# A self-attention block and a channel-correlation norm on one core: the second image's products moved into image 0, a third tile split on GpSimd, and the last image finished in three column pieces

## The chip, the cores and the metric

One core of one Trainium2 chip. The metric is the device time of one execution in microseconds (us), taken over repeated runs. TensorE (PE) does the matmuls, VectorE (DVE), ScalarE (ACT) and GpSimd (POOL) the rest, SyncE (SP) issues most DMAs.

## The reference

The input has 8 images of 128 channels by 1024 pixels, in float32.

```python
x_f = einsum('oc,bcn->bon', Wf, xf) + bf      # 16 x 1024, as x_g; x_h is 128 x 1024
s = einsum('bci,bcj->bij', x_f, x_g)          # 1024 x 1024 an image
beta = softmax(s, axis=-1)
y = x + gamma * einsum('bci,bij->bcj', x_h, beta)
x_n = y / max(norm(y over pixels), 1e-12)
cos = einsum('bcn,bdn->cd', x_n, x_n) / B     # needs all 8 images
idx = top_k(-abs(cos), 4)                     # per channel, 3 partners beside itself
# sums and squares over a channel and its partners give mean and var of each image
out = gn_gamma * (y - mean) * rsqrt(var + 1e-5) + gn_beta
```

## The kernel before, in words

**Tiles and slots.** An image is 8 row tiles of the score matrix (T = 8, 128 rows each, 1024 columns in two halves of 512, one PSUM bank each). Image b, tile t is slot 8b + t. In a slot TensorE issues the scores of the tile four slots ahead (`AHEAD`, `score`, L633) into one of two PSUM buffers `s_ps`, then `attend` (L654) for its own tile: the product of the values and the tile's softmax rows, added up over the 8 tiles in `o_ps`. VectorE takes each row's maximum (`row_max`, L408), ScalarE the exponential with its row sum (`exp`, L329), VectorE the reciprocal of that sum (L412). As `s_ps` has two buffers, the scores of a tile wait for the exponential of the tile two before it.

**Whole and split tiles.** A tile is used in one of two forms. Whole: ScalarE scales the 128 x 128 values by the reciprocal (`vnorm`, L342), and TensorE does one float32 product a half, which the trace shows as two passes. Split: rows and values are each written as a high and a low float32r part, and TensorE does three float32r products a half. `VECTOR_SPLIT` (3, 6) are made by ScalarE (high, L338) and VectorE (low, L417: two inputs in SBUF); `POOL_SPLIT` (2, 7) by GpSimd alone in three instructions (scale L266, cast L269, subtract L271), three slots ahead of their use. GpSimd also splits the values of the next image (L257, L259), in two halves, and raises the norms to -1/2 (L277, L284). Its queue goes in slot order: tile 7, the norm, the values, then the next image's tile 2.

**What else stands in the slots of image b.** f and g of image b+1 (`project_fg`, L606, both halves, slots 0 and 1), cut into parts by ScalarE (`negate_high`, L322, both in slot 0) and VectorE (`parts`, L425); a DMA turns the g half to other partitions (`g_low`, L229). The values of image b+1 (`project_values`, L615, slots 4 and 5). Of image b-1: its transposes (L671, slots 2 and 3), copies of them (L354, L455), its squares (L347), its gram product (L676, slot 6), scaling, a transpose of the gram (L686) and its addition to `half_cos` (L471). The two residuals (L448) close an image. All these places are constants by hand, `PE_FG` to `DVE_ADD`. Every engine runs its list in order; semaphores join them.

**Start and end.** Ahead of slot 0 TensorE does image 0's f, g and values and four scores. After the last slot the last image goes through its residual, transposes, copies, gram, norm, scaling, turn and sum one after the other (L519 to L545), then come the choice of partners, mean and variance (L545 to L564), the scaling of all images (L395, L399, L579, L583) and the stores.

## Time and profile before

| what | value |
|---|---|
| median of 3 runs | 213.71 us (213.17 to 214.1) |
| the profiled execution's own time | 213.46 us |
| its span, first to last instruction | 211.7 us |
| mean granted TensorE clock | 0.944 of full |
| busy: PE, DVE, ACT, POOL | 87%, 77%, 63%, 52% of the span |
| HBM read, written | 4.52 MB, 4.19 MB |

Busy time of an engine is the union of its records. A matmul's record is longer than the step to the next one (pipelining), so costs on TensorE are read from the chain of waits, where pieces follow each other without overlap. The chain goes back from the last instruction, at each step to what released it.

### The profile page before, as it was taken

What the parts mean: (1) busy time and instruction counts of PE and PEld (TensorE: products, weight loads), DVE (VectorE), ACT (ScalarE), POOL (GpSimd) and SP (SyncE); (2) the same over time, 40 slices, a digit from 0 to 9 for tenths busy, and PEclk for the clock granted to TensorE, in tenths of its full rate; (3) what the DMA queues carried; (4) which work ended last, traced back from release to release, by engine and by line L of the source; (5) the groups of instructions that cost most, each with busy time, mean ns of one, the idle gap of its engine ahead of it and who ended that gap; (6) DMA issues with size and microseconds to landing.
All of it is one profiled execution on the core that took longest, in us unless ns stands there. A gap on an engine that the chain in (4) does not pass through costs nothing.

```text
span 211.7 us, 2461 instructions
## 1 busy us (share of the span) xinstructions
PE 184.7 (87%) x759; PEld 122.7 (58%) x759; DVE 162.3 (77%) x283; ACT 133.5 (63%) x231; POOL 109.1 (52%) x106
## 2 busy tenths in 40 slices
PE   7949999999999999999999999999999999872000
PEld 3614567667766776577757775777576756541000
DVE  1594889799788988898889888988898886366640
ACT  2267484689648964896589757985698478240420
POOL 4007519922993199419940995099608971910400
PEclk9975999999999999999999999999999999998555
DMA  5300050013000400050005000200020000000297
GB/s 200 159 0 0 0 152 0 0 28 124 0 3 12 136 0 0 0 152 0 2 2 152 0 0 2 50 0 0 3 50 0 0 5 0 0 0 0 104 401 290
DMA packets 4013, 10.71 MB, mean 51 GB/s; under 512 B 544, under 2 KB 672, under 8 KB 4000
## 3 DMA queue, kind: packets, MB, share of 16 engines
q1 hardware_dynamic: 3424, 9.18, 13.4%
q10 hardware_dynamic: 576, 1.38, 1.8%
q8 instruction: 6, 0.10, 0.2%
q14 instruction: 7, 0.06, 0.1%
HBM read 4.52 MB, written 4.19 MB: 41 GB/s over the span
## 4 chain that ended last, share of the span: by engine, by line
PE 74%; DVE 11%; POOL 4%; ACT 3%; issue 3%; DVEq 0%; ACTq 0%; POOLq 0%
PE o_ps L654 41%; PE s_ps L633 13%; PE w_ps L606 6%; PE w_ps L615 6%; DVE nmax L408 3%; PE w_ps L676 3%; PE w_ps L671 3%; PE o_ps L590 2%; ACT probs L329 1%; DVE x_all L583 1%; POOL probs_low L271 1%; DVE fg_parts L425 1%; POOL probs_high L269 1%; DVE probs_low L417 1%; DVE g_low L432 1%
## 5 line engine op out<-in xcount | busy, mean ns | idle before, releaser
L329 ACT ACTIVATE probs<-s_ps,nmax 128x1024 f32<-128x1024 f32 x64 | 71.4, 1115 | 39.4 <-DVE nmax L408 39.4
L408 DVE TENSOR_REDUCE nmax<-s_ps 128x1 f32<-128x1024 f32 x64 | 77.9, 1219 | 12.1 <-PE s_ps L633 12.1
L266 POOL TENSOR_SCALAR probs<-probs,rinv 128x1024 f32<-128x1024 f32 x16 | 24.3, 1522 | 74.2 <-DVE rinv L412 73.5
L654 PE MATMUL o_ps<-probs,vnorm 128*128 128x512 f32 x128 | 60.8, 598 | 0.4 <-DVE x_all L448 0.4
L633 PE MATMUL s_ps<-g_low,fg_parts 128*128 128x512 f32 x128 | 50.6, 478 | 4.1 <-ACT probs L329 3.4
L271 POOL TENSOR_TENSOR probs_low<-probs,probs_high 128x1024 fp32r<-128x1024 f32 x16 | 38.1, 2382 | 1.4
L654 PEld LDWEIGHTS o_ps<-probs,vnorm 128*128 128x128 f32 x128 | 24.5, 192 | 22.8 <-issue 19.2
L633 PEld LDWEIGHTS s_ps<-g_low,fg_parts 128*128 128x128 f32 x128 | 21.2, 194 | 15.2 <-issue 7.7
L654 PE MATMUL o_ps<-probs_high,v_high 128*128 128x512 f32 x64 | 25.3, 396 | 0.8 <-POOL probs_low L271 0.8
L654 PE MATMUL o_ps<-probs_high,v_low 128*128 128x512 f32 x64 | 25.2, 394 | 0.0
L654 PE MATMUL o_ps<-probs_low,v_high 128*128 128x512 f32 x64 | 25.0, 391 | 0.0
L417 DVE SCALAR_TENSOR_TENSOR probs_low<-probs,rinv,probs_high 128x1024 fp32r<-128x1024 f32 x16 | 21.9, 1366 | 2.0 <-ACT probs_high L338 1.4
L322 ACT ACTIVATE fg_neg<-w_ps,bias_neg,wd 128x512 fp32r<-128x512 f32 x16 | 12.3, 772 | 10.7 <-PE w_ps L606 10.7
L269 POOL CAST probs_high<-probs 128x1024 fp32r<-128x1024 f32 x16 | 18.3, 1145 | 1.0
L615 PEld LDWEIGHTS w_ps<-wd,x_all 128*128 128x128 f32 x112 | 14.7, 192 | 6.7 <-issue 6.7
L338 ACT ACTIVATE probs_high<-probs,rinv 128x1024 fp32r<-128x1024 f32 x16 | 18.3, 1144 | 0.0
L606 PE MATMUL w_ps<-x_all,wd 128*128 128x512 f32 x32 | 18.2, 659 | 0.0
L615 PE MATMUL w_ps<-wd,x_all 128*128 128x128 f32 x112 | 14.8, 275 | 0.0
L654 PEld LDWEIGHTS o_ps<-probs_high,v_high 128*128 128x128 f32 x64 | 12.0, 187 | 4.5 <-issue 1.8
L654 PEld LDWEIGHTS o_ps<-probs_low,v_high 128*128 128x128 f32 x64 | 12.0, 188 | 2.8
L654 PEld LDWEIGHTS o_ps<-probs_high,v_low 128*128 128x128 f32 x64 | 12.0, 188 | 2.6
L425 DVE SCALAR_TENSOR_TENSOR fg_parts<-w_ps,wd,fg_neg 128x512 fp32r<-128x512 f32 x16 | 11.9, 747 | 1.0 <-ACT fg_neg L322 0.8
(88 smaller groups left out, 200.8 us busy)
## 6 DMA issues: line engine op xcount, KB each, us to landing
x_all<-x_dram SPq DMA_DIRECT2D x7, 512.0 KB, 3.5
out_dram<-x_all SPq DMA_DIRECT2D x5, 512.0 KB, 6.6
g_low<-fg_parts SPq DMA_DIRECT2D x14, 128.0 KB, 2.2
out_dram<-x_all ACTq DMA_DIRECT2D x2, 512.0 KB, 4.9
x_all<-x_dram SPq DMA_DIRECT2D x2, 256.0 KB, 3.8
out_dram<-x_all SPq DMA_DIRECT2D x2, 256.0 KB, 2.2
wd<-wide_dram ACTq DMA_DIRECT2D x1, 256.0 KB, 4.7
wd<-wide_dram ACTq DMA_DIRECT2D x1, 66.5 KB, 3.4
```

Of the source, the lines that this page charges most:

```text
L266: nc.gpsimd.tensor_scalar(probs[t][:, :], probs[t][:, :], rinv[:, t:t + 1], 1.0, ALU.mult, ALU.mult).then_inc(pool_scaled, 1)
L269: nc.gpsimd.tensor_copy(probs_high[n][:, :], probs[t][:, :]).then_inc(pool_high, 1)
L271: nc.gpsimd.tensor_tensor(probs_low[n][:, :], probs[t][:, :], probs_high[n][:, :].bitcast(F32), ALU.subtract).then_inc(pool_low, 1)
L329: nc.scalar.activation(probs[t][:, :], s_ps[t % 2][:, :], ACT.Exp, bias=nmax[:, t:t + 1], accum_out=rsum[:, t:t + 1]).then_inc(exp_done, 1)
L338: nc.scalar.activation(probs_high[SPLIT.index(t)][:, :], probs[t][:, :], ACT.Copy, scale=rinv[:, t:t + 1]).then_inc(high_ready, 1)
L408: nc.vector.reduce_max(nmax[:, t:t + 1], s_ps[t % 2][:, :], AX_X, negate=True).then_inc(max_ready, 1)
L417: nc.vector.scalar_tensor_tensor(probs_low[n][:, :], probs[t][:, :], rinv[:, t:t + 1], probs_high[n][:, :].bitcast(F32), ALU.mult, ALU.sub ...
L425: nc.vector.scalar_tensor_tensor(fg_parts[b % 2][:, halves[h]], w_ps[:, halves[h]], wd[:, BFG:BFG + 1], fg_neg[:, halves[h]].bitcast(F32), ...
L606: nc.tensor.matmul(w_ps[:, halves[h]], wd[:, WFG:WFG + P], x_all[:, b, halves[h]], start=True, stop=True).then_inc(fg_proj, 1)
L615: last = nc.tensor.matmul(to[:, t * P:(t + 1) * P], x_all[:, b, t * P:(t + 1) * P], wd[:, WHT:WHT + P], start=True, stop=True)
L633: last = nc.tensor.matmul(s_ps[t % 2][:, h], fg_parts[b % 2][:, t * P:(t + 1) * P], g_low[b % 2][:, h], start=True, stop=True)
L654: last = nc.tensor.matmul(o_ps[:, halves[h]], weights, rows[:, halves[h]], start=(t == 0 and n == 0), stop=(t == T - 1 and n == len(produc ...
```

## The change

f and g of image 1 are made before slot 0, between the first scores, with four idle matmuls ("fills") ahead of them; for that image 0's first parts are made in pieces. GpSimd splits tiles 2, 4 and 7 of images 1 to 6; image 0 has 6 (VectorE), 4 and 7 (GpSimd); the last image 1 and 3 (GpSimd). The values of image b+1 are both made in slot 5, the transposes both in slot 2, the squares in slot 3. In the last image `attend` goes over all tiles three times, for 512, 256 and 256 columns; its transposes and its gram (float32, no parts) are interleaved with the later pieces, its norm is applied by a product with a diagonal matrix and by a factor of the sum, and the other images' sum is finished meanwhile. The mean's square is taken by ScalarE. The rest is bookkeeping of the counts. The diff, cut to its core:

```diff
 AHEAD = 4
+NEAR = 3
...
-POOL_SPLIT = (2, 7)
-SPLIT = (2, 3, 6, 7)
+POOL_SPLIT = (2, 4, 7)
+FIRST_VECTOR, FIRST_POOL = (6,), (4, 7)
+LAST_VECTOR, LAST_POOL = (), (1, 3)
...
-PE_V, DVE_V, POOL_V = (4, 5), (5, 5), (5, 6)
-PE_T, ACT_T, DVE_T = (2, 3), (1, 3), (3, 4)
-ACT_SQUARE, POOL_NORM = 4, 4
+PE_V, DVE_V, POOL_V = (5, 5), (5, 5), (5, 6)
+PE_T, ACT_T, DVE_T = (2, 2), (1, 3), (3, 4)
+ACT_SQUARE, POOL_NORM = 3, 4
+HALF_TURN, LAST_T, LAST_G = 1, (3, 3), (4, 7)
+FILLS = 4
...
+        PIECES = [slice(0, BANK), slice(BANK, BANK + 2 * P), slice(BANK + 2 * P, N)]
+        PIECE_TILES = [range(0, TH), range(TH, TH + 2), range(TH + 2, T)]
+        def split_values_of(b, h):
+            its = [t for t in range(h * TH, (h + 1) * TH) if is_split(b, t)]
+            if not its:
+                return None
+            gaps = {n - m for m, n in zip(its, its[1:])}
+            return slice(its[0], its[-1] + 1, gaps.pop() if len(gaps) == 1 else 1)
...
-            square_half(0)
-            act.wait_ge(gram_made, L)
-            for h in range(H):
-                act.wait_ge(yT_made, H * L + 1 + h)
-                nc.scalar.activation(yT[:, h * TH:(h + 1) * TH, 0:P],
-                                     s_ps[h][:, halves[0]].rearrange("p (t c) -> p t c", c=P),
-                                     ACT.Copy).then_inc(yT_high, 1)
-            square_half(1)
+            square_piece(0)
+            copy_piece(0, s_ps[0][:, halves[0]])
+            square_piece(1)
+            copy_piece(1, s_ps[0][:, BANK:BANK + 2 * P])
+            square_piece(2)
+            act.wait_ge(mom_made, 1)
+            nc.scalar.activation(msq[:, :], o_ps[:, BANK:BANK + B], ACT.Square).then_inc(msq_ready, 1)
...
             first_g(0)
-            parts(0, 0)
+            first_parts(slice(0, 2 * P), parts_first)
             first_g(1)
-            parts(0, 1)
+            first_parts(slice(2 * P, BANK), parts_ready)
...
+                if slot == 1 - AHEAD:
+                    parts(0, 1)
...
-            for h in range(H):
-                low_yT(L, h, s_ps[h][:, halves[0]])
             if DVE_ADD >= T:
                 add_gram(L - 1, w_ps[:, BANK:BANK + P])
-            scale_gram(L, o_ps)
...
+            last_residual(0, o_ps[:, halves[0]], sums[:, 0, L:B])
+            nc.vector.tensor_scalar(half_mean[:, :], half_cos[:, :], 1.0 / B, None, ALU.mult).then_inc(last_ready, 1)
+            nc.vector.scalar_tensor_tensor(whole_cos[:, :], w_ps[:, BANK:BANK + P], 1.0 / B, half_mean[:, :],
+                                           ALU.mult, ALU.add).then_inc(last_ready, 1)
+            last_residual(1, o_ps[:, PIECES[1]], sums[:, 1, L:B])
+            last_residual(2, w_ps[:, 0:2 * P], last_sum[:, 0:1])
+            nc.vector.tensor_copy(last_yT[:, PIECES[2]], s_ps[1][:, BANK:BANK + 2 * P])
+            dve.wait_ge(rnorm_ready, B)
+            nc.vector.tensor_scalar(norms[:, :], ident, rnorm[:, L:B], 1.0 / B, ALU.mult, ALU.mult)
+            dve.wait_ge(gram_made, B)
+            nc.vector.tensor_copy(last_gram[:, :], s_ps[1][:, 0:P])
...
-            step(nc.vector.scalar_tensor_tensor(cos[:, :], s_ps[0][:, BANK:BANK + P], 1.0 / B, half_mean[:, :],
+            step(nc.vector.scalar_tensor_tensor(cos[:, :], o_ps[:, 0:P], rnorm[:, L:B], whole_cos[:, :],
                                                 ALU.mult, ALU.add))
...
-            for slot in range(-AHEAD, T * B):
+            score(0, 0)
+            score(0, 1)
+            pe.wait_ge(parts_ready, 1)
+            for _ in range(FILLS):
+                nc.tensor.matmul(w_ps[:, halves[0]], warm[:, 0:P], warm[:, :], start=True, stop=True)
+            project_fg(1, 0)
+            score(0, 2)
+            project_fg(1, 1)
+            done = 3
+            for slot in range(0, T * B):
+                due = slot + (AHEAD if slot + AHEAD > NEAR else AHEAD - 1)
+                while done <= min(due, T * B - 1):
+                    score(*divmod(done, T))
+                    done += 1
...
-                if slot >= 0:
+                if b < L:
                     attend(b, t)
+                else:
+                    if t == 0:
+                        pe.wait_ge(y_ready, H * L)
+                    attend_piece(t, 0, o_ps[:, halves[0]])
...
+            for t in range(T):
+                attend_piece(t, 1, o_ps[:, PIECES[1]])
+                if t == HALF_TURN:
+                    pe.wait_ge(gram_added, B)
+                    nc.tensor.transpose(w_ps[:, BANK:BANK + P], half_cos[:, :], ident)
+                if t == LAST_T[0]:
+                    last_transposes(0, s_ps[0][:, halves[0]])
+            for t in range(T):
+                attend_piece(t, 2, w_ps[:, 0:2 * P])
+                if t == LAST_G[0]:
+                    last_gram_piece(0)
+                if t == LAST_T[1]:
+                    last_transposes(1, s_ps[0][:, BANK:BANK + 2 * P])
+                if t == LAST_G[1]:
+                    last_gram_piece(1)
+            last_transposes(2, s_ps[1][:, BANK:BANK + 2 * P])
+            last_gram_piece(2)
+            pe.wait_ge(last_scaled, 2)
+            nc.tensor.matmul(o_ps[:, 0:P], last_gram[:, :], norms[:, :], start=True, stop=True)
```

`attend_piece` issues the products of one tile for one piece; `last_residual`, `square_piece` and `copy_piece` are L448, L382 and L389 of before for a piece's columns.


## Rows read from the trace of the kernel before

**Rows 1.** The page: busy time of each engine, share of the span, instructions.

```profile
PE 184.7 (87%) x759; PEld 122.7 (58%) x759; DVE 162.3 (77%) x283; ACT 133.5 (63%) x231; POOL 109.1 (52%) x106
```

**Rows 2.** Chain of waits: start us, us, what; images 1 and 2.

```profile
39.46 0.86 PE w_ps L606 x2
...
46.94 0.44 PE w_ps L671 x4
...
49.68 0.47 PE s_ps L633 x2
...
57.68 0.95 PE w_ps L676 x8
...
60.57 0.47 PE s_ps L633 x2
...
74.77 1.72 PE o_ps L654 x4
...
80.64 1.37 PE o_ps L654 x6
...
82.12 0.47 PE s_ps L633 x2
```

**Rows 3.** Windows view, one image: busy time by engine, then clock.

```profile
60.50:82.00 21.50, 21.50 (x95) 14.84 (x94) 18.66 (x32) 16.01 (x28) 13.07 (x13) 1.00 0.14 37
```

**Rows 4.** Timeline of image 0: start us, us, engine, line [idle before <-releaser].

```profile
9.79 1.20 PE L633 MATMUL s_ps<-g_low,fg_parts 128*128 128x512 f32 x4 [0.42 <-DVE g_low L432]
...
16.36 1.22 PE L633 MATMUL s_ps<-g_low,fg_parts 128*128 128x512 f32 x2 [0.94 <-ACT probs L329]
...
24.76 0.78 ACT L322 ACTIVATE fg_neg<-w_ps,bias_neg,wd 128x512 fp32r<-128x512 f32 x1 [2.97 <-PE w_ps L606]
...
38.85 0.61 PE L633 MATMUL s_ps<-g_low,fg_parts 128*128 128x512 f32 x2
```

**Rows 5.** Windows view of the start: TensorE's granted clock is the PEclk column.

```profile
14.00:15.00 1.00, 0.80 (x2) 0.50 (x2) 1.00 (x2) 0.44 (x3) 0.00 (x0) 0.50 0.00 0
...
20.00:21.00 1.00, 1.00 (x3) 0.47 (x2) 0.00 (x0) 1.00 (x2) 1.00 (x1) 0.75 0.00 0
```

**Rows 6.** Timeline of GpSimd, with one VectorE row it collides with.

```profile
23.37 0.73 POOL L259 TENSOR_TENSOR v_low<-values,v_high 128x256 fp32r<-128x256 f32 x1
...
23.40 1.78 DVE L417 SCALAR_TENSOR_TENSOR probs_low<-probs,rinv,probs_high 128x1024 fp32r<-128x1024 f32 x1
...
51.57 2.19 POOL L266 TENSOR_SCALAR probs<-probs,rinv 128x1024 f32<-128x1024 f32 x1 [7.82 <-DVE rinv L412]
...
57.44 0.23 POOL L277 TENSOR_SCALAR nsq<-stats 128x1 f32<-128x1 f32 x1
...
58.76 0.74 POOL L259 TENSOR_TENSOR v_low<-values,v_high 128x256 fp32r<-128x256 f32 x1
...
60.75 1.12 POOL L266 TENSOR_SCALAR probs<-probs,rinv 128x1024 f32<-128x1024 f32 x1
...
63.06 2.37 POOL L271 TENSOR_TENSOR probs_low<-probs,probs_high 128x1024 fp32r<-128x1024 f32 x1
...
179.01 1.12 POOL L266 TENSOR_SCALAR probs<-probs,rinv 128x1024 f32<-128x1024 f32 x1 [5.82 <-DVE rinv L412]
...
184.65 0.22 POOL L277 TENSOR_SCALAR nsq<-stats 128x1 f32<-128x1 f32 x1
```

**Rows 7.** Timeline of the last image, from the wait for its last tile on.

```profile
184.71 0.47 PE L654 MATMUL o_ps<-probs_high,v_high 128*128 128x512 f32 x1 [0.80 <-POOL probs_low L271]
...
186.95 0.75 DVE L448 SCALAR_TENSOR_TENSOR x_all<-o_ps,wd,x_all 128x512 f32<-128x512 f32 x1
...
188.95 0.62 ACT L382 ACTIVATE squares<-x_all 128x512 f32<-128x512 f32 x1
...
190.15 0.55 POOL L284 TENSOR_TENSOR rnorm<-nsq,mhalf 128x1 f32<-128x1 f32 x1
...
192.81 0.29 DVE L543 SCALAR_TENSOR_TENSOR cos<-s_ps,half_mean 128x128 f32<-128x128 f32 x1 [0.24 <-PE s_ps L739]
```

More of the change, by code:

```diff
@@ L180, in build, with vector_split, pool_split, is_split @@
         GROUPS = [slice(0, 1), slice(1, 3), slice(3, B)]
-        WHOLE = [t for t in range(T) if t not in SPLIT]
-        def split_values_of(h):
-            its = [t for t in SPLIT if t // TH == h]
-            step = its[1] - its[0] if len(its) > 1 and len({b - a for a, b in zip(its, its[1:])}) == 1 else 1
-            return slice(its[0], its[-1] + 1, step)
-        SPLIT_VALUES = [split_values_of(h) for h in range(H)]
+        PIECES = [slice(0, BANK), slice(BANK, BANK + 2 * P), slice(BANK + 2 * P, N)]
+        PIECE_TILES = [range(0, TH), range(TH, TH + 2), range(TH + 2, T)]
+        def vector_split(b):
+            return FIRST_VECTOR if b == 0 else LAST_VECTOR if b == L else VECTOR_SPLIT
+        def pool_split(b):
+            return FIRST_POOL if b == 0 else LAST_POOL if b == L else POOL_SPLIT
+        def is_split(b, t):
+            return t in vector_split(b) or t in pool_split(b)
+        def split_values_of(b, h):
[4 more added lines that the diff above has]
+            return slice(its[0], its[-1] + 1, gaps.pop() if len(gaps) == 1 else 1)
         def shifts_for(b):
@@ L289, in _ @@
                 its = tile_at(slot + AHEAD - 1)
-                if its is not None and its[1] in POOL_SPLIT:
+                if its is not None and its[1] in pool_split(its[0]):
                     split_probs(*its)
@@ L496, in _ @@
                     add_gram(i, w_ps[:, BANK:BANK + P])
-                if t == T - 1 and b >= 0:
+                if t == T - 1 and 0 <= b < L:
                     residual(b, 0)
                     residual(b, 1)
+                if slot == 1 - AHEAD:
+                    parts(0, 1)
                 its = tile_at(slot + AHEAD - LOW_LAG)
-                if its is not None and its[1] in VECTOR_SPLIT:
+                if its is not None and its[1] in vector_split(its[0]):
                     low_part(*its)
@@ L659, in attend, with attend_piece @@
                 last.then_inc(probs_used, 1)
+            def attend_piece(t, piece, to):
+                products = products_of(L, t)
+                for n, (weights, rows) in enumerate(products):
+                    last = nc.tensor.matmul(to, weights, rows[:, PIECES[piece]], start=(t == 0 and n == 0),
+                                            stop=(t == T - 1 and n == len(products) - 1))
+                if t == T - 1:
+                    last.then_inc(last_products, 1)
             def transposes(b, h, to):
@@ L672, in transposes, with gram, last_transposes, last_gram_piece @@
                 last.then_inc(yT_made, 1)
-            def gram(to, tiles):
-                for t in tiles:
+            def gram(to):
+                for t in range(T):
                     last = nc.tensor.matmul(to[:, 0:2 * P], yT[:, t, 0:P], yT[:, t, :], start=(t == 0),
                                             stop=(t == T - 1))
+                return last
+            def last_transposes(n, to):
+                pe.wait_ge(y_ready, H * L + 1 + n)
+                for at, t in enumerate(PIECE_TILES[n]):
+                    last = nc.tensor.transpose(to[:, at * P:(at + 1) * P], x_all[:, L, t * P:(t + 1) * P], ident)
+                last.then_inc(yT_made, 1)
+            def last_gram_piece(n):
+                if n < 2:
+                    pe.wait_ge(last_copied, n + 1)
+                else:
+                    pe.wait_ge(last_end, 1)
+                for t in PIECE_TILES[n]:
+                    rows = last_yT[:, t * P:(t + 1) * P]
+                    last = nc.tensor.matmul(s_ps[1][:, 0:P], rows, rows, start=(t == 0), stop=(t == T - 1))
                 return last
@@ L696, in _ @@
                 project_values(0, h, o_ps)
-            for slot in range(-AHEAD, T * B):
+            score(0, 0)
[8 more added lines that the diff above has]
+            for slot in range(0, T * B):
                 b, t = divmod(slot, T)
-                its = tile_at(slot + AHEAD)
-                if its is not None:
-                    score(*its)
+                due = slot + (AHEAD if slot + AHEAD > NEAR else AHEAD - 1)
+                while done <= min(due, T * B - 1):
+                    score(*divmod(done, T))
+                    done += 1
                 for h in range(H):
-                    if 0 <= b < L and t == PE_FG[h] == 0:
+                    if 0 < b < L and t == PE_FG[h] == 0:
                         project_fg(b + 1, h)
@@ L723, in _ @@
                         pe.wait_ge(v_ready, H * (i + 2) + 1)
-                    gram(w_ps, range(T)).then_inc(gram_made, 1)
+                    gram(w_ps).then_inc(gram_made, 1)
                 i = before(b, t, PE_TURN)
```

173 lines of the change are left out of this document (110 added, 63 removed).

## The prediction

> **What bounds the kernel now.** I read the page first. TensorE is busy 184.7 of 211.7 us and no other engine comes near it [rows 1], but a busy share is a mean over stages, so I took the chain of waits next. From image 1 to image 6 it is TensorE alone: scores, products, f and g, values, transposes, gram, one behind the other without a gap. The scores of slot 16 start at 60.57 and those of slot 24 at 82.12 [rows 2], so an image takes 21.55 us. The window of that image confirms it: TensorE 21.50 of 21.50 us at full clock, VectorE 18.66, ScalarE 16.01, GpSimd 13.07 [rows 3]. Three stretches are left to gain in: the start, where TensorE waits or runs slowly; each middle image, where only less TensorE work helps, as long as no other engine falls behind; and the end, where the last image's steps follow each other.
>
> All sums go against the profiled execution: 213.46 us, its span of 211.7 and 1.76 around it. The median of the runs shown is 213.71, 0.1% above.
>
> **Start.** Score (0,4), of tile 4 of image 0, starts at 16.36, when exp(0,2) is done, and slot 8 starts at 38.85: 22.5 us for image 0 [rows 4]. Two things make it long. The clock is at its low level, 1.2 GHz, in 14 to 15 us and comes back to 2.4 GHz within 20 to 21 [rows 5]. And ScalarE waits 2.97 us, until 24.76, for the second half of image 1's f and g, which TensorE issues in slot 1 while ScalarE wants both in slot 0 [rows 4]; everything behind it, exp(0,5) first, is late.
>
> With the change f and g are done before slot 0. Up to score (0,4) two edits nearly cancel. The first parts are made in two pieces, so the second g starts about 0.3 earlier (a piece of 256 columns, my estimate 0.5 against 0.75 for one of 512 columns, the nearest row being the residual of that width [rows 7]), and so does the first score, at 9.5 instead of 9.79. But parts(0,1), 0.75, moves behind row_max(0,1), ahead of the first values and row_max(0,2), and costs about 0.6 there. Score (0,4) then starts at about 16.65. From there TensorE's own work to slot 8 is an image of 21.55, less f and g (2 x 0.86), transposes (2 x 0.44) and gram (0.95) with its turn (0.1), as image 0 has none [rows 2], plus 0.35 for one split tile fewer (three, before four): 18.25. Nothing ends later than TensorE in it: GpSimd's tile 4 starts at 21.0, takes 4.7 and is wanted at 25.8; the g half of image 1 reaches its partitions before it is wanted at 25.4. The fills and the two products lie in TensorE's idle time before 14.5. Slot 8 starts at 16.65 + 18.25 = 34.9 instead of 38.85: **-3.9**, if the clock stays up. TensorE's longest wait is now about 1.7 us, from score (0,3) to score (0,4), and it has worked more before it.
>
> **Images 1 to 6.** A whole tile costs TensorE 1.72, a split one 1.37 to 1.39 [rows 2]: tile 4 on GpSimd takes 0.33 off each image, 21.22, together -2.0. Moving the values, transposes and squares changes no sum on TensorE. Slots 3 and 4 now last 1.86 each; exp(6) must be done when score (b+1,0) starts, and by my count of the chain it is, by little. ScalarE loses one vnorm an image; VectorE's list is unchanged; DMAs are neither added nor moved, and g_low goes out in slot 1 as before, behind parts.
>
> The price is GpSimd's. Counted from the start of score (b+1,0), at 49.68 [rows 2], tile 7's scaling starts at +1.89 (51.57) and the norm behind it 5.64 to 5.87 later (179.01 to 184.65, and 51.57 to 57.44) [rows 6]. I take 5.64: GpSimd begins ahead of VectorE's low part there, and will do so again, because exp(7) and with it ScalarE's high part come later against slot 4. Then norm and the first half of the values, 2.06 (57.44 to the end of the subtraction at 59.50). The second half now spans tiles 4 to 7, four tiles instead of two: between 0.74 for 256 elements and 2.37 for 1024, the subtraction should take 1.28, with its cast 2.05. Tile 2 then takes 4.68 (60.75 to 65.43) and ends at +16.3; it is wanted at +17.1, so not late. But its subtraction is under way when VectorE's low part of tile 3 comes, at about +15.35. The rows at 23.37 and 23.40 show such a pair: the low part took 1.78, and ended 1.08 after GpSimd's 0.73 was over. So it waits for GpSimd's end and ends at +17.4, about 0.8 late; tile 4's scaling, in turn, waits for it, and tile 4 ends at about +21.9. TensorE wants it at 21.22 + 0.46 = +21.68. It waits w, and w counts twice, since the next image starts later too: 21.95 = 21.68 + 2w, w = 0.13; with 5.87 for tile 7, w = 0.25. In image 1 the way is tighter, as image 0 has no gram to give time: 0.4. Waits come to 1.05 to 1.65, and what is left of the 2.0 is 0.35 to 0.95; I take **-0.7**.
>
> The Trainium skill (SBUF — State Buffer, Who interferes with whom) says that VectorE with two SBUF inputs and GpSimd reading SBUF exclude each other for a whole instruction. It is the rule that speaks against this change: a subtraction of 2.37 would hold the low part off far longer than the 0.7 of the row. The trace agrees with it as far as one row of 0.73 can. If they shared the bandwidth instead, w would be nothing and the sum 1.3 better.
>
> **End.** Before, the last tile's products wait 0.80 us for GpSimd until 184.71 [rows 7]; one split tile of 1.4 and a step later, near 186.3, they end, and the correlation is formed at 192.81: 6.5 us for residual, transposes, copies, gram, norm, turn and sum. In the new order TensorE has more to do: six whole and two split tiles instead of four and four (+0.7), and two waits for GpSimd, since tile 1 is ready 3.7 after slot 56 and tile 3 another 4.7 later (about 0.75 and 1.3 us), and 0.6 for both residuals of image 6 ahead of slot 56. Without exponentials left to hide it these count in full. Piece 0 then ends near 181.7 on the old time axis, pieces 1 and 2 take 3.3 each with 0.5 and 0.7 of transposes and gram between them: the last product near 189.3, 3.0 later than before. Behind it only a short chain is left: residual of 256 columns 0.5 (from 0.75), square 0.6 with its sum (from 0.8), two GpSimd steps 0.95 (the second 0.55), the diagonal 0.3, the copy 0.3, a product 0.35, and hand-overs: 3.2 instead of 6.5 [rows 7]. The correlation is at about 192.5 instead of 192.81, and ScalarE's square of the mean saves 0.1 to 0.2: **-0.4**. The transposes and the gram of piece 2 run beside the norm and end before it; if the norm were faster, they would be next, 0.7 behind. What follows, scaling and stores, is the same instructions. Ends of this term: +0.8, if GpSimd's tile 1 is another 1.2 late, and -1.5, if it waits for neither.
>
> **Sum.** 213.46 - 3.9 - 0.7 - 0.4 = 208.5 us.
>
> **The rivals.** (a) *The clock falls in the second gap.* Before, it fell after TensorE had nothing from 10.99 (9.79 + 1.20) until exp(0,0) was done [rows 4]; now 1.7 us without work stand before score (0,4), with a product and two scores ahead. If it falls there and comes back at about 20.5 as before [rows 5], TensorE does half its work in 3.9 us: +1.9, 210.4. The fills help only the first gap. For it: 14.5 to 16.6 looks like the old gap; against it: the work before. The Trainium skill (TensorE: Matmul & The Clock Gate, Part 1) says the low clock is the default and activity releases it; that allows either. (b) *GpSimd isn't late.* If the low part is held less, or tile 4 comes in time, images 1 to 6 give all 2.0, and the last image's waits shrink by about 0.3: 206.9. (c) *The end gives nothing or costs*, by its upper end: 209.7. (d) *GpSimd becomes the bound, and the kernel is slower.* Its place is tile 4, wanted in slot 4. If VectorE's parts and residuals (four a image, 0.75 each) held it off too, its way would be 3.0 longer, w = 1.6 and an image 22.85 instead of 21.55: +7.8 against the 4.3 of start and end, 217.0. It decides from 22.3 an image on. Against it: the scaling at 60.75 took its shortest, 1.12, with image 1's residuals beside it. The same section of the Trainium skill says that VectorE with one SBUF input does not contend. That the change doesn't do what it says can hardly be: the counts and places are plain in the diff.
>
> **Chances.** Forecast 0.45 (its own range 207.3 to 209.7), (a) 0.24, (b) 0.14, (c) 0.11, (d) 0.06. The range leaves out (d) and the outer half of (b) and reaches over (a): 206.5 to 211.2. What a measurement of this kernel can tell from no change is about 0.5%, 1.1 us: faster by more than that 0.90, within it 0.04, slower 0.06.
>
> **What would show it.** Right: scores of slot 8 near 34.9; granted clock 1.00 from 9 to 35 us; ScalarE without a wait for f and g; scores 21.3 to 21.5 us apart from image to image, with short waits of TensorE for GpSimd's subtraction; low parts of tile 3 near 2.1 us and of tile 6 near 1.4; GpSimd busy about 20 us an image; the correlation 3.2 us behind the last product. Wrong: 0.50 in the clock between 15 and 20 us (a); images 21.2 apart (b); the last product over 4 us later against slot 56 than before (c); images over 22.3 apart (d).

## The result, and the profile after

The changed kernel takes 211.68 us (median of 4 runs, 210.68 to 211.99) against 213.91 of the kernel before beside it: ratio 0.9892, 95% interval 0.9847 to 0.9937. It is faster, by 2.2 us where 5.0 were forecast, and the time lies above the range. The profiled execution is the shortest of the four, 210.68 with a span of 208.9. The first rows of its page (busy time, then two rows of the slices), which answer to [rows 1]:

```profile
PE 183.1 (88%) x796; PEld 125.9 (60%) x796; DVE 162.2 (78%) x281; ACT 130.9 (63%) x228; POOL 143.3 (69%) x121
...
POOL 4003869988999699979996999799969992001400
PEclk9999999999999999999999999999999999997555
```

GpSimd has 34 us more to do, as meant, and the clock stays up from the first slice. What the page says of the chain that ended last, by engine and by line:

```profile
PE 43%; POOL 36%; DVE 12%; issue 3%; ACT 1%; DVEq 0%; POOLq 0%; ACTq 0%
PE o_ps L738 19%; POOL probs_low L313 14%; POOL probs L308 8%; POOL probs_high L311 8%; PE s_ps L716 6%; DVE nmax L460 5%; PE o_ps L749 4%; POOL v_low L301 3%; PE w_ps L687 3%; PE w_ps L696 3%; PE w_ps L769 2%; PE o_ps L670 2%; PE w_ps L749 2%; POOL v_high L299 1%; DVE x_all L663 1%
```

Before, TensorE held 74% of this chain and GpSimd 4%. Now a third of the span hangs on GpSimd, though no single wait for it is long.

Four marks cut both profiled executions into terms (slot 8 and slot 56 are the starts of their scores, the correlation is the instruction that forms it):

| stretch | before | after | difference | forecast |
|---|---|---|---|---|
| start to slot 8 | 38.85 | 34.98 | -3.87 | -3.9 |
| slot 8 to slot 56 (images 1 to 6) | 129.24 | 129.25 | 0.0 | -0.7 |
| slot 56 to the correlation | 24.72 | 25.84 | +1.12 | -0.3 |
| correlation to the end of the span | 18.9 | 18.8 | -0.1 | -0.1 |

The start came as forecast. The middle gave nothing, and the end cost 1.1. The timeline of image 0, which answers to [rows 4]:

```profile
9.43 1.19 PE L716 MATMUL s_ps<-g_low,fg_parts 128*128 128x512 f32 x4 [0.41 <-DVE g_low L488]
...
34.98 0.39 PE L716 MATMUL s_ps<-g_low,fg_parts 128*128 128x512 f32 x1
```

and the windows that answer to [rows 5]:

```profile
14.00:15.00 1.00, 1.00 (x4) 0.38 (x2) 1.00 (x2) 0.40 (x1) 0.00 (x0) 1.00 0.00 0
...
20.00:21.00 1.00, 1.00 (x4) 0.39 (x3) 0.77 (x2) 1.00 (x4) 0.13 (x1) 1.00 0.00 0
...
9.00:35.00 26.00, 23.72 (x88) 14.34 (x88) 23.21 (x34) 17.36 (x32) 13.54 (x12) 1.00 0.11 31
```

The granted clock is 1.00 in all of it (2.4 GHz), and no row of ScalarE waits for f and g any more.

In the middle image 1 is 21.92 long and the others 21.4 and 21.6 in turn, on average 21.54 as before. GpSimd's round, from the start of score (b+1,0) at 67.44 to the products of tile 4, with the low part of tile 3 that it collides with:

```profile
67.44 0.61 PE L716 MATMUL s_ps<-g_low,fg_parts 128*128 128x512 f32 x2
68.06 0.47 PE L738 MATMUL o_ps<-probs_high,v_high 128*128 128x512 f32 x1
...
69.49 1.12 POOL L308 TENSOR_SCALAR probs<-probs,rinv 128x1024 f32<-128x1024 f32 x1 [1.57 <-DVE rinv L464]
...
75.15 0.22 POOL L319 TENSOR_SCALAR nsq<-stats 128x1 f32<-128x1 f32 x1
...
77.15 0.61 POOL L299 CAST v_high<-values 128x512 fp32r<-128x512 f32 x1
77.84 1.29 POOL L301 TENSOR_TENSOR v_low<-values,v_high 128x512 fp32r<-128x512 f32 x1
...
79.22 1.12 POOL L308 TENSOR_SCALAR probs<-probs,rinv 128x1024 f32<-128x1024 f32 x1
...
81.53 2.36 POOL L313 TENSOR_TENSOR probs_low<-probs,probs_high 128x1024 fp32r<-128x1024 f32 x1
...
83.19 1.77 DVE L468 SCALAR_TENSOR_TENSOR probs_low<-probs,rinv,probs_high 128x1024 fp32r<-128x1024 f32 x1
...
83.86 2.10 POOL L308 TENSOR_SCALAR probs<-probs,rinv 128x1024 f32<-128x1024 f32 x1
...
87.14 2.40 POOL L313 TENSOR_TENSOR probs_low<-probs,probs_high 128x1024 fp32r<-128x1024 f32 x1
...
88.88 0.61 PE L716 MATMUL s_ps<-g_low,fg_parts 128*128 128x512 f32 x2
89.69 0.47 PE L738 MATMUL o_ps<-probs_high,v_high 128*128 128x512 f32 x1 [0.20 <-POOL probs_low L313]
```

Read it downwards: from tile 7's scaling on GpSimd has no gap. Its subtraction ends at 83.89; VectorE's low part, begun at 83.19, ends 1.07 later at 84.96, and GpSimd's next scaling, begun at 83.86, ends at 85.96. Each is held while the other runs. TensorE gets tile 4 at 89.69, 22.25 after 67.44. From the start of the scores to the first product of tile 4 it takes 0.62 in one image (67.44 to 68.06) and 0.81 in the next (88.88 to 89.69), where 0.46 would be without a wait.

The last image, timeline of TensorE with the steps that answer to [rows 7]:

```profile
165.91 1.12 PE L749 MATMUL o_ps<-probs,vnorm 128*128 128x512 f32 x2 [0.97 <-DVE x_all L504]
...
168.18 0.47 PE L749 MATMUL o_ps<-probs_high,v_high 128*128 128x512 f32 x1 [0.68 <-POOL probs_low L313]
...
172.83 0.47 PE L749 MATMUL o_ps<-probs_high,v_high 128*128 128x512 f32 x1 [1.05 <-POOL probs_low L313]
...
178.75 0.74 DVE L579 SCALAR_TENSOR_TENSOR x_all<-o_ps,wd,x_all 128x512 f32<-128x512 f32 x1
...
184.35 1.05 PE L787 MATMUL s_ps<-last_yT 128*128 128x128 f32 x8
...
185.25 1.46 PE L749 MATMUL w_ps<-probs,vnorm 128*128 128x256 f32 x6
...
186.75 0.48 DVE L579 SCALAR_TENSOR_TENSOR x_all<-w_ps,wd,x_all 128x256 f32<-128x256 f32 x1 [3.72 <-PE w_ps L749]
...
188.34 0.56 POOL L330 TENSOR_TENSOR rnorm<-nsq,mhalf 128x1 f32<-128x1 f32 x1
...
190.07 0.35 DVE L621 SCALAR_TENSOR_TENSOR cos<-o_ps,rnorm,whole_cos 128x128 f32<-128x128 f32 x1 [0.58 <-PE o_ps L879]
```

Three waits of TensorE (0.97, 0.68 and 1.05), 2.70 together, stand before tile 4. The residuals of pieces 0 and 2 start at 178.75 and 186.75. The gram of piece 0 (four tiles) begins at 184.35 and the next product at 185.25: 0.9 us. The chain of waits of the same stretch, where pieces don't overlap (start us, us, what):

```profile
178.14 0.30 PE w_ps L796
...
179.23 0.11 PE w_ps L860
...
184.52 0.89 PE s_ps L787 x8
```

Piece 0 ends at 178.14; the first row is the turn of image 6's gram, the second that of `half_cos`, the third the gram of piece 0. TensorE's last product of piece 2 ends at 186.72 in this chain.

### The profile page after: what moved, and what is told of

Its sections match the earlier page's. It is cut to its first block, busy times and chain, and to the rows that moved or that the text cites. A ratio compares the mean times of both kernels' runs of the same rounds, so it can differ in the third digit from the quotient of the medians.

```text
span 208.9 us, 2554 instructions
## 1 busy us (share of the span) xinstructions
PE 183.1 (88%) x796; PEld 125.9 (60%) x796; DVE 162.2 (78%) x281; ACT 130.9 (63%) x228; POOL 143.3 (69%) x121
## 4 chain that ended last, share of the span: by engine, by line
PE 43%; POOL 36%; DVE 12%; issue 3%; ACT 1%; DVEq 0%; POOLq 0%; ACTq 0%
PE o_ps L738 19%; POOL probs_low L313 14%; POOL probs L308 8%; POOL probs_high L311 8%; PE s_ps L716 6%; DVE nmax L460 5%; PE o_ps L749 4%; POOL v_low L301 3%; PE w_ps L687 3%; PE w_ps L696 3%; PE w_ps L769 2%; PE o_ps L670 2%; PE w_ps L749 2%; POOL v_high L299 1%; DVE x_all L663 1%
## 5 line engine op out<-in xcount | busy, mean ns | idle before, releaser
L375 ACT ACTIVATE probs<-s_ps,nmax 128x1024 f32<-128x1024 f32 x64 | 71.3, 1114 | 39.1 <-DVE nmax L460 38.9
L313 POOL TENSOR_TENSOR probs_low<-probs,probs_high 128x1024 fp32r<-128x1024 f32 x22 | 52.4, 2382 | 1.9
L716 PE MATMUL s_ps<-g_low,fg_parts 128*128 128x512 f32 x128 | 48.5, 461 | 2.1 <-ACT probs L375 1.7
L738 PE MATMUL o_ps<-probs,vnorm 128*128 128x512 f32 x92 | 43.2, 592 | 0.0
L308 POOL TENSOR_SCALAR probs<-probs,rinv 128x1024 f32<-128x1024 f32 x22 | 30.5, 1388 | 14.2 <-DVE rinv L464 13.6
L311 POOL CAST probs_high<-probs 128x1024 fp32r<-128x1024 f32 x22 | 28.9, 1312 | 1.4
L738 PEld LDWEIGHTS o_ps<-probs,vnorm 128*128 128x128 f32 x92 | 17.4, 189 | 15.3 <-issue 12.2
L468 DVE SCALAR_TENSOR_TENSOR probs_low<-probs,rinv,probs_high 128x1024 fp32r<-128x1024 f32 x13 | 23.6, 1813 | 2.7 <-ACT probs_high L384 2.7
L299 POOL CAST v_high<-values 128x512 fp32r<-128x512 f32 (+1 forms) x14 | 7.1, 505 | 13.3 <-DVE values L495 13.3
L301 POOL TENSOR_TENSOR v_low<-values,v_high 128x512 fp32r<-128x512 f32 (+1 forms) x14 | 14.2, 1013 | 1.1
L384 ACT ACTIVATE probs_high<-probs,rinv 128x1024 fp32r<-128x1024 f32 x13 | 14.8, 1139 | 0.0
```

The lines of the kernel that those rows point to most:

```text
L301: nc.gpsimd.tensor_tensor(v_low[b % 2][:, tiles, :], source, v_high[b % 2][:, tiles, :].bitcast(F32), ALU.subtract).then_inc(vl_ready, 1)
L308: nc.gpsimd.tensor_scalar(probs[t][:, :], probs[t][:, :], rinv[:, t:t + 1], 1.0, ALU.mult, ALU.mult).then_inc(pool_scaled, 1)
L311: nc.gpsimd.tensor_copy(probs_high[t][:, :], probs[t][:, :]).then_inc(pool_high, 1)
L313: nc.gpsimd.tensor_tensor(probs_low[t][:, :], probs[t][:, :], probs_high[t][:, :].bitcast(F32), ALU.subtract).then_inc(pool_low, 1)
L375: nc.scalar.activation(probs[t][:, :], s_ps[t % 2][:, :], ACT.Exp, bias=nmax[:, t:t + 1], accum_out=rsum[:, t:t + 1]).then_inc(exp_done, 1)
L384: nc.scalar.activation(probs_high[t][:, :], probs[t][:, :], ACT.Copy, scale=rinv[:, t:t + 1]).then_inc(high_ready, 1)
```

## The experiments

Each is the changed kernel but for the edit shown. Times are medians. The ratio is to the kernel before, measured beside each: 213.26 us beside the first four; 213.58 beside "two tiles and the old end", "tile 1", "tile 5" and "the last image without its three waits"; 213.46 beside "less of the values", "half of the gram" and "the changed kernel again"; 213.40 beside the last. Distances in images are taken between first residuals in the profiled execution.

**The start put back.** Order and pieces of the start as before, the rest as changed.

```
-            first_parts(slice(0, 2 * P), parts_first)
+            parts(0, 0)
-            first_parts(slice(2 * P, BANK), parts_ready)
+            parts(0, 1)
...
-            for _ in range(FILLS):
-                nc.tensor.matmul(w_ps[:, halves[0]], warm[:, 0:P], warm[:, :], start=True, stop=True)
-            project_fg(1, 0)
-            score(0, 2)
-            project_fg(1, 1)
```

> The changed kernel with the start of before: image 1's f and g in slots 0 and 1, no fills, first parts in two halves. Theory (the start gave all of the gain): slot 8 starts 3.9 later, at about 38.9 instead of 34.98, the distances from slot to slot behind it stay, and the whole is 3.9 slower than the changed kernel, thus slightly slower than before: 214.6 profiled against 210.68 and 213.46. Rival (what the start gives is taken back behind it, since the other engines then bound the images): less than 2 slower than the changed kernel.

214.59, ratio 1.0064 (1.0047 to 1.0081). The first residual of image 0, just before slot 8, is at 38.1 instead of 35.03; the images lie 21.95 to 21.37 apart as in the changed kernel. A row of its windows and one of its timeline:

```profile
14.00:15.00 1.00, 1.00 (x3) 0.45 (x2) 0.92 (x1) 0.19 (x1) 0.00 (x0) 0.50 0.00 0
```

```profile
24.37 0.78 ACT L368 ACTIVATE fg_neg<-w_ps,bias_neg,wd 128x512 fp32r<-128x512 f32 x1 [2.88 <-PE w_ps L684]
```

The low clock of 1.2 GHz and ScalarE's wait are back. The start's new order is worth about 3 us, not the 3.9 expected. Image 0 keeps its new plan (three split tiles instead of four, values in slot 5) in this run, and 0.8 us of the gain stays with it (first residual at 38.1, in the kernel before at 38.9). How those 0.8 divide was not tested. Without the new order the change is slower than before: middle and end together cost.

**No fills.**

```
-FILLS = 4
+FILLS = 0
```

> The changed kernel without the four idle matmuls. Theory (f and g of image 1 alone keep TensorE busy enough): granted clock stays 1.00 up to slot 8 and the time stays within 0.5 of the changed kernel. Rival (the fills are what holds the clock): 0.50 somewhere between 13 and 21 us and slot 8 up to 1.9 later.

210.49, ratio 0.9859 (0.9836 to 0.9883). The granted clock is 1.00 in every microsecond from 9 to 24 here too: in this kernel f and g alone were enough, and the fills bring nothing. One image was 23.08 long, for this row of its timeline:

```profile
89.94 0.70 PE L716 MATMUL s_ps<-g_low,fg_parts 128*128 128x512 f32 x2 [1.66 <-DMA g_low<-fg_parts]
```

Of the 14 transfers of g_low one took 4.2 us to land instead of 2.2 in this run, and TensorE waited.

**Two tiles on GpSimd.**

```
-POOL_SPLIT = (2, 4, 7)
+POOL_SPLIT = (2, 7)
```

> The changed kernel with tile 4 of images 1 to 6 whole again (GpSimd splits 2 and 7). Theory (TensorE saves 0.33 an image by the third tile and then waits about as long for GpSimd): images 21.55 apart without a wait of TensorE, slot 56 within 0.3 of its 164.2, the whole within 0.5 of the changed kernel, and GpSimd back at 61 to 63% busy or less. Rival 1 (the third tile is worth its 0.33 an image, and the moved values and transposes cost something): slot 56 at 166.2, the whole 2 slower. Rival 2 (the third tile costs more than it saves, through VectorE's blocked low parts): the whole 1 or more faster.

209.83, ratio 0.983 (0.9802 to 0.9857). Images are 21.50 apart, and no wait of TensorE stands between slots 8 and 56. So the third tile, meant to save 0.33 an image, saves nothing. The run is faster than the changed kernel by more than the 0.5 expected, 0.9 between the profiled executions. The interval of its ratio lies below that of the changed kernel's repetition further down (0.9862 to 0.9938), not quite below that of the first measurement. So the rival that the third tile costs isn't excluded; but in the profiles images 1 to 6 give only 0.3 of the 0.9, and 0.45 is image 0, where both kernels are the same.

**The end put back.** Last image in halves, its gram and correlation as before, its splits as before, (3, 6) on VectorE and (2, 7) on GpSimd.

```
-LAST_VECTOR, LAST_POOL = (), (1, 3)
+LAST_VECTOR, LAST_POOL = (3, 6), (2, 7)
...
-            for t in range(T):
-                attend_piece(t, 1, o_ps[:, PIECES[1]])
```

> The changed kernel with the end of before (one pass over the last image, tiles 2, 3, 6, 7 split as before, then residual, transposes, copies, gram, norm, turn one after the other). Theory (the pieces cost more TensorE time than they hide): from slot 56 to the correlation 24.7 us as before, not the 25.8 of the changed kernel, so 1.1 faster than it: 209.6 profiled. Rival (the pieces are needed now, because GpSimd is late into the last image with three tiles an image): 26 or more from slot 56 to the correlation, no faster than the changed kernel.

209.89, ratio 0.9857 (0.9796 to 0.9918). From the first residual of image 6 to the correlation: 24.82, against 25.63 in the changed kernel. The new end costs 0.8. The kernel before took 24.51 for it, so 0.3 of the 1.12 comes from what this edit leaves changed; it was not traced.

**Two tiles and the old end**, both edits above together.

> The changed kernel with tile 4 whole again and the end of before: of the change only the start, the moved values, transposes and squares, and image 0's plan stay. Theory (third tile and pieces each cost, and the two add up): from the first residual of image 0 to that of image 6 129.1 us (21.50 an image), from there to the correlation 24.5 to 24.8; profiled 209.0, about 0.8 below each of the two single undoings, and the fastest of all so far. Rival (they don't add up; the piecewise end is only dear because three tiles an image leave GpSimd late): the correlation 25.6 after the last residual of image 6, and no gain over the kernel with two tiles and the new end, 209.8.

209.39 (209.12 to 209.69), ratio 0.9805 (0.9774 to 0.9836), images 21.50 apart, 24.80 to the correlation. The two undoings leave the start's gain alone, and its runs lie within 0.6.

**Tile 1 instead of tile 3 on VectorE**, against the collision.

```
-VECTOR_SPLIT = (3, 6)
+VECTOR_SPLIT = (1, 6)
```

> The changed kernel with VectorE and ScalarE splitting tiles 1 and 6 instead of 3 and 6; GpSimd keeps 2, 4 and 7. The same number of split tiles, the same work on each engine, but no low part of VectorE falls between GpSimd's tiles 2 and 4. Theory (the lock between the low part and GpSimd's subtraction makes tile 4 late): tile 4 in time, 21.2 to 21.3 an image, 1.5 faster than the changed kernel: 209.2 profiled, and low parts of tile 1 blocked for less. Rival 1 (GpSimd's own work is the bound, lock or not): still 21.5. Rival 2 (the low part in slot 7 delays row maxima and blocks GpSimd's tile 2 instead): 21.6 or more.

214.32, ratio 1.0032 (1.0009 to 1.0054), images 22.1 to 22.6 apart. Timeline of TensorE, two of its waits:

```profile
63.91 0.47 PE L738 MATMUL o_ps<-probs_high,v_high 128*128 128x512 f32 x1 [0.34 <-POOL probs_low L313]
...
68.89 0.70 PE L716 MATMUL s_ps<-g_low,fg_parts 128*128 128x512 f32 x2 [0.31 <-DMA g_low<-fg_parts]
```

Tile 4 is now in time, but VectorE's low part of tile 1 falls on GpSimd's tile 2 and takes 2.08, and tile 2 is late in every image. The collision was moved. The wait for g_low is another matter: it comes once, in the image that is 22.6 long, where the transfer landed after 3.8 us instead of 2.2.

**Tile 5 instead of tile 4 on GpSimd.**

```
-POOL_SPLIT = (2, 4, 7)
+POOL_SPLIT = (2, 5, 7)
```

> The changed kernel with GpSimd splitting tiles 2, 5 and 7 instead of 2, 4 and 7; VectorE as it is. Tile 5 is wanted one slot (1.9 us) later than tile 4. Theory (TensorE only loses because tile 4's subtraction ends 0.3 late): no wait of TensorE at that tile; but tile 5's work of 4.7 us now runs into tile 7's, whose start moves back by about 1, so at best 21.2 to 21.4 an image. Rival (GpSimd's queue has no room wherever the third tile stands): 21.5 or more, with the wait at tile 2 or 7 instead.

216.57, ratio 1.0141 (1.0103 to 1.0179), images 22.47 apart. Its timeline:

```profile
71.47 2.08 POOL L308 TENSOR_SCALAR probs<-probs,rinv 128x1024 f32<-128x1024 f32 x1
71.62 0.47 PE L738 MATMUL o_ps<-probs_high,v_high 128*128 128x512 f32 x1 [0.79 <-POOL probs_low L313]
...
78.23 0.35 DVE L518 TENSOR_SCALAR gram_high<-w_ps,rnorm 128x128 f32<-128x128 f32 x1 [1.26 <-POOL rnorm L330]
```

TensorE waits 0.79 for tile 5 itself, in every image from 2 on, which neither the theory nor its rival had. Tile 7 has to stand behind tile 5, and the norm behind tile 7. This is what rival (d) of the prediction looks like: over 22.3 an image the kernel is slower than before.

**Less of the values on GpSimd.** From image 2 on the parts of the second half of the values are made for tiles 4 and 7 alone; those of tile 6 are left out.

```
+                if b >= 2 and h == 1:
+                    tiles = slice(TH, T, TH - 1)
```

> The changed kernel, but from image 2 on GpSimd makes the high and low parts of the second half of the values for tiles 4 and 7 alone (two tiles of values instead of four), which leaves the values of tile 6 with old parts; this work is left out. In the changed kernel the cast and the subtraction of the four tiles take 2.01 us together. Theory of the loop (tile 7's scaling, norm, values, tile 2, the low part of tile 3, tile 4 follow each other, and 2w = 22.24 - 21.68 = 0.56 is what they are late): two tiles take about 1.25, so 0.75 less stands in the loop, more than the 0.56 it is late; images 21.2 to 21.3 apart instead of 21.5, no wait of TensorE for GpSimd's subtraction in slot 4, the run 1.2 to 1.8 faster than the changed kernel. Rival (VectorE's own queue holds the images: its low parts of 2 us push row maxima and g_low late): still 21.5 apart, within 0.4 of the changed kernel.

209.12, ratio 0.9799 (0.976 to 0.9837). The windows of the same image in both, the changed kernel first, then a row of this run's timeline:

```profile
78.34:99.97 21.63, 21.43 (x97) 15.20 (x96) 19.39 (x33) 15.93 (x27) 19.38 (x16) 1.00 0.14 37
```

```profile
77.71:98.94 21.23, 21.23 (x97) 15.26 (x96) 19.05 (x34) 15.84 (x27) 18.51 (x16) 1.00 0.13 38
```

```profile
82.57 1.28 DVE L470 SCALAR_TENSOR_TENSOR probs_low<-probs,rinv,probs_high 128x1024 fp32r<-128x1024 f32 x1
```

From image 2 on they are 21.23 to 21.27 apart, with no wait of TensorE for GpSimd, and VectorE's low part of tile 3 takes 1.28 (last row) instead of 1.53 to 1.80, since tile 2's subtraction is over when it comes. That settles the middle: GpSimd's list was late, by less than the 0.77 taken out (0.61 + 1.29 to 0.40 + 0.73), and TensorE's own image is 21.25. VectorE's queue, the rival, holds nothing. The run is 2.2 faster than the changed kernel beside it. In the profiles images 1 to 6 take 128.2 us, against 129.4 and 130.6 in the two of the changed kernel; the longer one has a wait of 0.92 for a late g_low in it.

**The last image without its three waits.** Two tiles as above; the last image has one split tile, 2, on GpSimd, and its first products wait for the first residual of image 6 only.

```
-LAST_VECTOR, LAST_POOL = (), (1, 3)
+LAST_VECTOR, LAST_POOL = (), (2,)
...
-                        pe.wait_ge(y_ready, H * L)
+                        pe.wait_ge(y_ready, H * L - 1)
...
+            pe.wait_ge(y_ready, H * L)
             for t in range(T):
                 attend_piece(t, 1, o_ps[:, PIECES[1]])
```

> Two GpSimd tiles in images 1 to 6, the new end, but in the last image only tile 2 split, and its first products wait for the first residual of image 6 alone. It takes away TensorE's three waits ahead of tile 4 (0.97, 0.68 and 1.05 us in the changed kernel) and adds 0.35 of TensorE work. Theory of the prediction (these waits count in full): the correlation 23.3 after image 6's first residual, 2.3 less than with two tiles and the new end (25.6). Rival (ScalarE's chain of exponentials, with copies and squares among them, ends just behind and holds the last tiles anyway): 25.1 to 25.6.

210.24, ratio 0.9824 (0.978 to 0.9868), and 25.56 from the first residual of image 6 to the correlation, where two tiles alone have 25.57 (23.3 was expected by the theory, 25.1 to 25.6 by the rival). The waits in its timeline are now these:

```profile
168.06 0.73 PE L716 MATMUL s_ps<-g_low,fg_parts 128*128 128x512 f32 x2 [0.61 <-ACT probs L375]
...
169.22 0.47 PE L749 MATMUL o_ps<-probs_high,v_high 128*128 128x512 f32 x1 [0.42 <-POOL probs_low L313]
...
174.33 1.12 PE L749 MATMUL o_ps<-probs,vnorm 128*128 128x512 f32 x2 [0.27 <-ACT vnorm L388]
```

With the 0.30 that is left of the wait for image 6 they come to 1.60 instead of 2.65, but piece 0's residual starts only 0.17 earlier and the correlation not at all. Part of what was taken away came back as waits for exponentials, for the tile that is left and for ScalarE's scaled values. The chain of waits of this run shows what holds TensorE instead: it goes from the turn of image 6's gram at 177.66 back over VectorE's scaling, GpSimd's norm and ScalarE's copy and squares to the last exponentials. That is the chain that the rival named.

**Half of the gram of piece 0**, two of its four tiles left out.

```
-                for t in PIECE_TILES[n]:
+                for t in (range(2) if n == 0 else PIECE_TILES[n]):
```

> The changed kernel, but the gram of the last image's first column piece is made of two of its four tiles; this leaves half of that piece's gram out. The four float32 products take 0.89 us in the changed kernel. Theory (once ScalarE's chain has let the first piece go, TensorE is the bound behind it, so its products count in full): 0.45 less, and the correlation starts 25.4 instead of 25.84 behind the first residual of image 6. Rival (the products lie beside the residual of piece 1 and cost nothing): 25.84 unchanged.

(The 25.84 and 25.4 in it count from slot 56's score, not from the residual.) 211.24, ratio 0.9877 (0.9841 to 0.9913). From the residual of piece 0 to the correlation it is 10.88, in the changed kernel 11.32 in both of its profiled executions: 0.44 less, all of what was left out. So TensorE bounds that stretch. One g_low landed after 4.2 us here, and that image took 23.11.

**The changed kernel again**, unaltered.

> The changed kernel once more, unaltered, beside the two others. Theory (the spread of its runs is made by landings of g_low that come late now and then, as in the run without fills): median 211 to 212 with single runs 1 to 2 apart, in the profile images 21.4 to 21.65 apart, or one near 23 with a wait of TensorE for the DMA that brings g_low. Rival (the spread is the start's, the first projection's DMA): images as before and the first residual of image 0 moved by up to 0.8 from run to run.

211.36 (210.81 to 212.25), ratio 0.99 (0.9862 to 0.9938). Both explanations of the spread have something for them. Its profiled execution, 210.92, has a landing of 3.5 us, a wait of 0.92 and an image of 22.3, and it still ends near the first profile because its image 0 was 0.68 earlier (first residual at 34.35 instead of 35.03).

**Piece 1 beside the exponentials.** Two tiles as above; TensorE multiplies piece 1 of tile t-1 ahead of piece 0 of tile t, instead of all of piece 1 behind piece 0. The transposes of piece 0 then stand behind tile 1 of piece 2. No work is left out.

```
+                    if t > 0:
+                        attend_piece(t - 1, 1, o_ps[:, PIECES[1]])
                     attend_piece(t, 0, o_ps[:, halves[0]])
...
-            for t in range(T):
-                attend_piece(t, 1, o_ps[:, PIECES[1]])
...
+            attend_piece(T - 1, 1, o_ps[:, PIECES[1]])
...
                 attend_piece(t, 2, w_ps[:, 0:2 * P])
+                if t == 1:
+                    pe.wait_ge(exp_done, T * B)
+                    last_transposes(0, s_ps[0][:, halves[0]])
```

> The changed kernel with GpSimd splitting tiles 2 and 7 (as in the earlier run), and in the last image TensorE multiplies the second column piece of tile t-1 ahead of the first piece of tile t, in the same slot, where in the changed kernel all of the second piece stands behind the first; the last tile's second piece and the turn of half_cos follow piece 0, the transposes of piece 0 stand behind tile 1 of piece 2. Nothing is left out. In the run with two tiles TensorE is busy for 11.59 of the 14.24 us between the first residual of image 6 and that of piece 0, so 2.65 are idle, and piece 1 of seven tiles is about 2.9 us of work. Theory (the new end costs because TensorE has only half of the columns to do beside the last exponentials, and the rest stands behind them): the work goes into the idle time, piece 0 ends 0.3 to 0.9 later, the last product 2.0 to 2.6 earlier, from the first residual of image 6 to the correlation 23.0 to 23.6 instead of 25.57, the run 207.2 to 207.9 against 209.83, faster than both kernels and than the two tiles with the old end (209.39). Rival (the chain of maxima and exponentials is fed by TensorE's scores, and each piece put ahead of them delays it by as much): piece 0 ends 2 to 3 later and the correlation moves by less than 0.6.

208.67 (208.22 to 209.21), ratio 0.9779 (0.975 to 0.9807): the shortest median of all, and faster than both kernels; its interval overlaps with that of two tiles and the old end (0.9774 to 0.9836). From the first residual of image 6 to the correlation: 24.39, where 23.0 to 23.6 was expected, 25.57 with two tiles alone and 24.80 with two tiles and the old end. The windows of that stretch to piece 0's residual, cut where TensorE gets tile 3, for two tiles alone and for this kernel:

```profile
163.67:172.30 8.63, 5.98 (x25) 3.48 (x24) 6.79 (x16) 6.26 (x13) 7.91 (x5) 1.00 0.00 1
172.30:177.91 5.61, 5.61 (x23) 3.23 (x22) 2.37 (x6) 3.23 (x7) 0.79 (x2) 1.00 0.01 3
```

```profile
163.86:172.49 8.63, 7.21 (x33) 4.60 (x32) 6.45 (x14) 6.09 (x12) 7.90 (x5) 1.00 0.00 1
172.49:179.55 7.06, 7.06 (x31) 4.57 (x29) 2.71 (x8) 3.39 (x8) 0.79 (x2) 1.00 0.01 2
```

The first part lasts 8.63 in both, so the 1.23 us of products in it were free; the gain is 1.18. In the second part TensorE had no idle time, and products put there count in full (1.45), so piece 0 ends 1.45 later, not 0.3 to 0.9. The theory is right in kind, its 2.0 to 2.6 too large: it took all 2.65 idle us as fillable, and 0.96 of them stand before any product of the last image exists; another 0.45, in two waits for GpSimd, stayed unfilled.

## Why the prediction was wrong

Two terms failed. In images 1 to 6 it is the wait w for GpSimd's tile 4: it came out at 0.28 instead of 0.13, and with image 1's wait and TensorE's own 21.25 an image (said: 21.22) it took all of the 0.7 that was forecast. At the end it is TensorE's own work in the new order, 19.8 us instead of 18.6, above all the gram and the turns between the pieces: the end cost 1.1 where it should have given 0.4.

**Start, right.** -3.87 against -3.9: slot 8 at 34.98 against 34.9. Score (0,4) starts at 16.53 (said: 16.65), and from there to slot 8 it is 18.45 (said: 18.25). The clock did not fall, so rival (a) is out. That the sum agrees to 0.03 is luck: in the twelve profiles with f and g ahead of slot 0 the first residual of image 0 lies anywhere from 34.3 to 35.3. With the start put back the run is 3 us slower.

**Images 1 to 6: the mechanism was right, the sum too small.** The form 21.68 + 2w, with w the wait for tile 4, holds: the round took 22.25 instead of 21.95, so w = 0.28 instead of 0.13 (half of what two neighbouring images wait together: the rows show 0.16 in one and 0.35 in the next, and the images are 21.4 and 21.6 long in turn). Of the extra 0.3, 0.16 lies in tile 7's scaling, at +2.05 instead of +1.89, and 0.15 in the hand-over from GpSimd's end to TensorE, which the sum had left out. Its other terms were right: 5.66 for tile 7, 2.06 and 2.01 for the values, a low part of tile 3 that ends at +17.5 (said: +17.4). The rule that stood against the change (the Trainium skill, SBUF — State Buffer, Who interferes with whom) is borne out by the rows: the low part did not share with a subtraction of 2.36, it ended 1.07 after it. As 1.07 is less than the 1.28 of a low part alone, some 0.2 of it was done before. But from image 2 on that low part took 1.53 to 1.80, not 2.1, since it came later, and tile 6's took 1.86, not 1.4. With TensorE's own 21.25 (the run with fewer values) w = 0.28 gives 21.53; images 2 to 6 are 21.50 apart on average. Image 1 was 21.92 long, 0.67 over TensorE's own 21.25, where 0.4 was said. The third tile saves 0.25 to 0.3 an image on TensorE and loses as much in waiting. Rival (b), GpSimd isn't late, is refuted, and (d) for this plan. The step that failed is the size of w: a bound that is 0.3 us from the next one was computed with terms good to 0.15.

**End, wrong.** +1.12 to the correlation and -0.1 behind it, instead of -0.4 in all. The three waits were forecast at 2.65 and measured at 2.70, which is closer than their parts (0.6, 0.75 and 1.3 against 0.97, 0.68 and 1.05), and the chain behind the last product at 3.2 and 3.35. What failed is what stands between. "Transposes and gram 0.5 and 0.7" took the gram's price from [rows 2], 0.95 for 8 tiles; but the new gram is formed from float32 values, and the four tiles of piece 0 took 0.9, twice the half of 0.95, and the run with half of it showed that it counts in full. In all TensorE needed 19.8 us without the waits from slot 56 to the end of the last product, where 18.6 were forecast. The chain splits the 1.2: 0.41 is this gram; 0.41 are the two turns (0.30 and 0.11), which the forecast did not have between the pieces; 0.2 is a slip of its own sum, 3.3 + 3.3 + 0.5 + 0.7 = 7.8 from 181.7 on, which it rounded to 189.3; and 0.25 lies before the end of piece 0 and was not split further; the transposes took 0.06 less than said. And "without exponentials left to hide it these count in full" is wrong for that stretch: exponentials are left there, the waits for GpSimd stand beside ScalarE's work, and taking 1.05 of them away brought nothing. They cost something only because the new order has nothing for TensorE to do meanwhile: it has half the columns of each tile to multiply beside the last exponentials, and keeps the other half for afterwards. Filled with piece 1, they gave back 1.18. (Of the +1.12, the undone end accounts for 0.8; 0.3 stays open.)

**The range.** Profile against profile the change is worth 2.78, between the medians 2.2. The term that the prediction did not have is a late landing of g_low: of the seven profiled executions with three tiles, the new start and the new end, four had one, of the seven others none. TensorE waited 0.3 to 1.7 us for it. That it makes up the other half microsecond of the medians is argued, not shown, since image 0 alone also varied, with its first residual between 34.35 and 35.03 in two profiles of the same kernel; and neither why a transfer lands late nor whether the third tile has to do with it was tried. Rival (c), the end costs, was the right one, at +0.8 still priced too low; with +1.1 for the end and nothing for the middle the sum is 213.46 - 3.9 + 1.1 = 210.7, the profiled time.

## What to carry to other kernels

Before work is moved to an engine off the critical path, write its round as a chain with every hand-over in it: here 0.3 us in 22 decided whether the 0.3 saved in each image arrives at all, and the plan with the shorter list was faster. In a pipeline's end, count what the bounding engine has to do beside the last steps of the others, not only what stands behind them: a step cut into pieces finishes early only if the other pieces fill the waits. And a wait that is removed is worth nothing until it is known what would be waited for next; here filling it gave 1.18 us and removing it nothing.

## What the runs showed of the hardware

GpSimd and VectorE held each other off in both directions, for nearly the whole of the instruction that was ahead: a low part of 1.28 took 1.77 and ended 1.07 after GpSimd's subtraction was over, a scaling of 1.12 took 2.10, a cast of 1.04 took 1.90. As it goes both ways, one meeting lengthened VectorE's list by 0.5 and GpSimd's by 1.0 us. TensorE's granted clock stayed at its upper level (1.00, 2.4 GHz) through image 0 with image 1's f and g in the first gap, with and without the four fills; with f and g taken back it was 0.50 from 13 to 19 us. Float32 products of 128 x 128 are recorded twice each in the gram (x8 for four tiles) and cost 0.22 us a tile. A transfer of g_low (128 KB) landed after 3.5 to 4.2 us instead of 2.2 in four of fourteen profiles, and TensorE waited 0.3 to 1.7 for it.
